# Graph network layer on one core: key, value and query products moved from the nodes in the last layer to the edges in attention

## Chip, cores and metric

One core of a Trainium2 chip runs the whole program in one launch. The metric is device time in microseconds, the median of a few runs; a profile is one more execution, read instruction by instruction. PE is the matrix engine, DVE the vector engine, ACT the scalar engine, POOL issues indirect transfers (gathers) and SP the plain ones.

## The reference, cut to what matters

```python
def L0(h, incidence, W_edge, b_edge, W_agg, b_agg):      # 3 rounds
    for _ in range(3):
        msgs = relu(take(h, src) @ W_edge + b_edge)
        agg = segment_sum(msgs, dst)
        h = relu(concat([agg, h]) @ W_agg + b_agg)
    return h
def L1(x, edge_index, edge_attr, ...):                   # H = 8 heads of C = 16
    q, k, v = x @ Wq + bq, x @ Wk + bk, x @ Wv + bv
    e = edge_attr @ We
    k_j, v_j = k[src] + e, v[src] + e
    logits = sum(q[dst] * k_j, axis=-1) / sqrt(C)
    ex = exp(logits - segment_max(logits, dst)[dst])
    agg = segment_sum(ex / denom[dst] * v_j, dst)
    h = ln(agg + x @ Wskip + bskip + x, g1, b1)
    return ln(gelu(h @ Wf1 + bf1) @ Wf2 + bf2 + h, g2, b2)
x = layernorm(x + L0(x, ...))
return layernorm(x + L1(x, edge_index, edge_attr_64, ...))
```

There are 50,000 nodes and 50,000 edges, sorted by dst; x has 128 columns, all fp32. Below, x1 is the x of the second-last line.

## The kernel before

The program runs in stages with a barrier between them: sorting, message passing (two rounds), the last layer (the third round and the first layer norm), a short table stage, attention, and feed-forward. A group is 512 rows (98 groups), a block 256 nodes (196 blocks).

`last_layer` works block by block. Each engine has a `turn(do)`: `do(-8, group(step))` runs step for the block 8 before the present one, and `group` only in every second block, which closes a group. Engines run their lists in order and meet only at semaphores (`reached` is a wait). POOL gathers message rows of 768 bytes, four tiles a group, into a ring of 32 tiles; DVE makes one-hot matrices (`hots`, three a block); PE adds the tiles by them (`add_tile`), adds the node's own product (L1157), transposes the sums (`turn_sums`, L1164); DVE adds x (`add_rows`, L1264: y, four buffers) and takes means and variances (`norm_stats`); ACT takes the root (`roots`, L1205), DVE makes scale and shift in five small operations (`deviations`, L1270 to L1280), ACT normalizes (L1212); PE transposes x1 (`turn_x1`, L1171), ACT copies the columns (L1219), and PE projects them to 384 columns, keys, values and queries, for each of four tiles (`project`, L1181 and L1182). Half of these go through DVE with the bias (`add_biases`, L1292), half through ACT (`evict`, L1225). SP stores x1 plus b2, the columns of x1, and kvq_rows of 1536 bytes a node.

`attention` works group by group, by `do(lag, step)` too. POOL gathers for each of four tiles of 128 edges the kvq row of src (`at_kv`) and the q part of dst's (`at_q`). PE makes the edge features in rows (`e_bank`), DVE adds keys and values, multiplies by q, and sums each head (`edge_logits`); ACT spreads the logits over the head's 16 columns, PE transposes them and the values. With edges along the free axis DVE then scans for the running maximum (`maxima`), `weigh`s the values, and scans numerator and denominator (`num_scan`, `den_scan`); PE transposes back (`turn_back`), DVE divides. PE also makes x1 @ (Wskip + I) here from the stored columns (`skip_product`), and between steps multiplies a constant tile (`keep_busy`, L1431), four products at three places of a turn, whose result is not used.

## Time and profile before

| | |
|---|---|
| Runs | 4398.65, 4410.13, 4412.01 us (median 4410.13) |
| Profiled execution, span from first to last instruction | 4405.3 us; this is the time of its own that the profile gives |
| Busy over the span | PE 3865.1, DVE 3498.7, POOL 2905.4, ACT 2233.6 us |
| Transferred | 878.32 MB, 199 GB/s on average |

Busy times overlap and are averages over stages with different limits; the same figures for one stage, and the order in time within one group, tell what that stage waits for. A matrix product's record includes its tail, so starts are compared with starts.

### The profile page before, as it was taken

The numbers are of one execution on the slowest core, as the hardware profiler recorded it, in microseconds if no ns is written. First come the engines' busy times: TensorE is split into PE (matmuls) and PEld (weight loads), VectorE is DVE, ScalarE is ACT, GpSimd is POOL, SyncE is SP. The second block draws the span as 40 slices with busy tenths as digits, with TensorE's granted clock in tenths as the row PEclk, the third lists the DMA queues.
The fourth block names the chain that finished last, engine by engine and source line by source line (L and its number), as shares of the span: only waits on it lengthen the run. The fifth ranks groups of instructions, "written<-read, shape, count | busy, mean of one in ns | idle before, by whom it ended". The sixth has DMA issues, their size and how long they took to land. (4 is left out here: it accounts for less than half of the span.)

```text
span 4405.3 us, 106270 instructions
## 1 busy us (share of the span) xinstructions
PE 3865.1 (88%) x21528; PEld 2669.2 (61%) x21627; DVE 3498.7 (79%) x11629; ACT 2233.6 (51%) x4904; POOL 2905.4 (66%) x2864
## 2 busy tenths in 40 slices
PE   5777769999899997999999788888889859999998
PEld 3555548878788886566666466666666634444443
DVE  7888857766567665788877689999999958999998
ACT  1333335555455553455554444444444437777777
POOL 3777767776477763655555177777777657777775
PEclk9999989999999999999999889888888979999999
DMA  2555558877578775788888667777777624444443
GB/s 88 174 176 176 176 162 244 246 234 235 183 241 244 236 234 177 263 303 301 293 298 283 236 192 207 204 205 208 207 207 203 186 86 125 132 126 132 126 131 94
DMA packets 610107, 878.32 MB, mean 199 GB/s; under 512 B 148009, under 2 KB 409232, under 8 KB 609932
## 3 DMA queue, kind: packets, MB, share of 16 engines
q1 hardware_dynamic: 490764, 631.93, 43.6%
q0 software_dynamic: 119168, 244.63, 21.5%
q14 instruction: 135, 1.11, 0.1%
q8 instruction: 40, 0.66, 0.1%
HBM read 477.60 MB, written 398.61 MB: 199 GB/s over the span
## 5 line engine op out<-in xcount | busy, mean ns | idle before, releaser
L798 POOL DMA_INDIRECT mp_gathered<-msg_rows,other_idx x784 | 754.6, 962 | 348.7 <-issue 198.8
L1120 POOL DMA_INDIRECT ll_gathered<-msg_rows,other_idx x392 | 385.0, 982 | 357.0 <-PE bank L1138 204.4
L816 PE MATMUL bank<-mp_edge_hot,mp_gathered 128*128 128x256 bf16 x3528 | 475.5, 275 | 34.5 <-POOLq L786 18.3
L560 POOL DMA_INDIRECT by_window<-so_pay,so_pos_i x392 | 387.1, 988 | 164.3 <-issue 111.3
L1713 POOL DMA_INDIRECT ff_agg<-at_rows,last_idx x392 | 383.2, 978 | 116.0 <-issue 105.9
L1415 POOL DMA_INDIRECT at_kv<-kvq_rows,kv_idx x392 | 377.2, 962 | 119.7 <-issue 112.4
L1417 POOL DMA_INDIRECT at_q<-kvq_rows,node_idx x392 | 376.5, 960 | 119.5 <-issue 117.1
L872 ACT ACTIVATE mp_h_out<-bank,mp_b_agg 128x256 f32<-128x256 f32 x392 | 185.9, 474 | 476.9 <-PE bank L834 469.6
L816 PEld LDWEIGHTS bank<-mp_edge_hot,mp_gathered 128*128 x3528 | 346.3, 98 | 104.4 <-issue 61.7
L905 DVE TENSOR_SCALAR mp_edge_hot<-digits,mp_first_col,column 128x256 bf16<-128x256 bf16 x1176 | 342.0, 359 | 66.5 <-issue 54.5
L928 DVE TENSOR_TENSOR mp_msg_out<-mp_rest,mp_msg_out 128x256 bf16<-128x256 f32 x392 | 166.8, 426 | 259.1 <-ACT mp_msg_out L885 255.4
L1825 PE MATMUL bank<-ff_h_cols,ff_w 128*128 128x512 f32 x784 | 371.2, 596 | 0.9 <-ACT ff_h_cols L1858 0.9
L1833 PE MATMUL bank<-ff_gelu,ff_w 128*128 128x512 f32 x784 | 369.6, 594 | 1.0 <-ACT ff_gelu L1865 1.0
L1431 PE MATMUL bank<-at_filler,ones 128*128 128x512 bf16 x1078 | 320.7, 421 | 20.2 <-issue 15.3
L1182 PE MATMUL bank<-ll_weights,ll_x_cols 128*128 128x384 f32 x784 | 323.5, 515 | 0.0
L1865 ACT ACTIVATE ff_gelu<-bank,ff_bf 128x512 f32<-128x512 f32 x392 | 262.5, 683 | 114.6 <-PE bank L1825 114.6
L1726 POOL TENSOR_TENSOR ff_rstd<-ff_eps_var,ff_half 128x12 f32<-128x12 f32 x104 | 239.4, 2302 | 107.7 <-DVE ff_eps_var L1749 104.0
L1825 PEld LDWEIGHTS bank<-ff_h_cols,ff_w 128*128 128x128 f32 x784 | 149.9, 191 | 189.9 <-issue 188.4
L1138 PE MATMUL bank<-ll_edge_hot,ll_gathered 128*128 128x256 bf16 x1764 | 236.6, 274 | 25.4 <-DVE ll_edge_hot L1245 23.4
L834 PE MATMUL bank<-mp_h_in,mp_w_agg_h 128*128 128x256 f32 x784 | 245.8, 396 | 9.3 <-issue 8.8
L845 PEld LDWEIGHTS bank<-mp_w_agg_a,mp_msg_cols 128*128 128x128 f32 x1568 | 237.9, 192 | 21.8 <-ACT mp_msg_cols L876 1.2
L845 PE MATMUL bank<-mp_w_agg_a,mp_msg_cols 128*128 128x128 f32 x1568 | 239.4, 275 | 0.9 <-DVE mp_rest L923 0.9
(267 smaller groups left out, 9434.1 us busy)
## 6 DMA issues: line engine op xcount, KB each, us to landing
msg_rows<-mp_msg_out SPq DMA_DIRECT2D x392, 192.0 KB
kvq_rows<-ll_proj SPq DMA_DIRECT2D x98, 768.0 KB
mp_h_in<-h_cols SPq DMA_DIRECT2D x392, 128.0 KB
h_cols<-mp_h_out SPq DMA_DIRECT2D x392, 128.0 KB
msg_rows<-so_msg_out SPq DMA_DIRECT2D x98, 384.0 KB
h_cols<-so_h_out SPq DMA_DIRECT2D x98, 256.0 KB
ll_h_in<-h_cols SPq DMA_DIRECT2D x196, 128.0 KB
x_rows<-ll_x_b SPq DMA_DIRECT2D x98, 256.0 KB
```

The source lines that it names most:

```text
L560: pool.indirect_dma_start(core.by_window, bass.IndirectOffsetOnAxis(ap=pos_i[k][:, t:t + 1], axis=0), pay[k][:, t, :], None, bounds_check= ...
L798: pool.indirect_dma_start(gathered[:, r * PARTS * D:(r + 1) * PARTS * D], None, core.msg_rows[layer % 2], bass.IndirectOffsetOnAxis(ap=cor ...
L816: product = nc.tensor.matmul(agg_bank[k], gathered[:, bass.ds(at + d * D, D)], hot, start=(first and d == 0), stop=True, skip_group_check= ...
L845: product = nc.tensor.matmul(msg_bank[r % 2][:, c * P:(c + 1) * P], msg_c[r % 2][:, c * P:(c + 1) * P], w_agg_a[:, :], start=True, stop=True)
L905: return nc.vector.tensor_scalar(to, core.digits[:, :], first_col[:, bass.ds(n, 1)], core.column[:, bass.ds(i, 1)], ALU.add, ALU.is_equal)
L1120: pool.indirect_dma_start(gathered[:, r * PARTS * D:(r + 1) * PARTS * D], None, core.msg_rows[(LAYERS - 1) % 2], bass.IndirectOffsetOnAxis ...
L1182: nc.tensor.matmul(proj_bank[t][:, 0:NPJ], x1_cols[q % 2][:, t * P:(t + 1) * P], weights[:, :], start=t < T - BY_ACT, stop=True, skip_grou ...
L1415: pool.indirect_dma_start(kv[g % DEEP][:, t, :], None, core.kvq_rows, bass.IndirectOffsetOnAxis(ap=core.kv_idx[:, at:at + 1], axis=0)).the ...
L1417: pool.indirect_dma_start(q[g % DEEP][:, t, :], None, core.kvq_rows.rearrange("n (a f) -> (n a) f", f=D), bass.IndirectOffsetOnAxis(ap=cor ...
L1713: pool.indirect_dma_start(agg[g % 4][:, t, :], None, core.at_rows, bass.IndirectOffsetOnAxis(ap=core.last_idx[:, at:at + 1], axis=0)).then ...
L1825: nc.tensor.matmul(hid_bank[c][:, :], w1[:, c * P:(c + 1) * P], h_c[k % 2][:, :], start=True, stop=True).then_inc(f1, 1)
L1833: product = nc.tensor.matmul(out_bank[k % 2][:, :], w2[:, c, :], act_c[c][:, :], start=(c == 0), stop=(c == FC - 1))
```

## The change

The last layer no longer projects to keys, values and queries. Its place is taken by the skip product, which came from attention; x1 is stored without b2, its columns are no longer stored. `roots` and `deviations` run once for two groups (`pair`), and normalization and what follows it run two groups later. Attention gathers rows of x1 (512 bytes) for src and for dst, transposes them on PE, and makes keys, values and queries for each edge with edges along the free axis: keys and values each as two accumulating products (`with_edges`, x1 of src and edge attributes). DVE multiplies keys plus bias by queries (`products`), and one product with a 0/1 matrix of heads (`logits`) sums each head and spreads the sum. `keep_busy` is gone. DVE also adds b2 to x1 here and SP stores it for the feed-forward stage. The decay goes to SBUF instead of PSUM. The rest of the stages is unchanged but for the names of tensors.

```diff
+        def pair(step):
+
+            def at_fourth_block(n, r, j):
+                if r % 4 == 3:
+                    step(PAIRS * j + r // 4, r // 4)
+            return at_fourth_block
+
         words = {}
...
             def store(g):
-                k = g % 2
-                reached(sp, xb2_ok, g + 1)
-                sp.dma_start(rows(core.x1_rows, g), x1_b2[k][:, :, :]).then_inc(st_x1[k], 16)
-                reached(sp, cols_ok, g + 1)
-                sp.dma_start(core.x1_cols[:, g * GR:(g + 1) * GR], x1_cols[k][:, :]).then_inc(st_cols[k], 16)
-                reached(sp, by_act, BY_ACT * (g + 1))
-                reached(sp, by_dve, (T - BY_ACT) * (g + 1))
-                sp.dma_start(rows(core.kvq_rows, g), proj[k][:, :, :]).then_inc(st[k], 16)
+                reached(sp, x1_ok, g + 1)
+                sp.dma_start(rows(core.x1_rows, g), x1[g % Q][:, :, :]).then_inc(st_x1[g % Q], 16)
+                reached(sp, skip_ok, g + 1)
+                sp.dma_start(rows(core.skip_rows, g), skip[g % 2][:, :, :]).then_inc(st_skip[g % 2], 16)
 
             for n in range(RING - 1):
                 load_h(n)
...
+            def skip_product(g, q, j):
                 pe.wait_ge(cols_ok, g + 1)
+                reached(pe, skip_ok, g - 1)
+                nc.tensor.matmul(skip_bank[q % 2][:, :], core.ones[0:PARTS, :], skip_parts[:, :], start=True, stop=True, skip_group_check=True)
                 for t in range(T):
-                    if t < T - BY_ACT:
-                        reached(pe, by_dve, (T - BY_ACT) * (g - 1) + t + 1)
-                    else:
-                        reached(pe, by_act, BY_ACT * (g - 1) + t - (T - BY_ACT) + 1)
-                        nc.tensor.matmul(proj_bank[t][:, 0:NPJ], core.ones[0:PARTS, :], proj_parts[:, :], start=True, stop=True, skip_group_check=True)
-                    nc.tensor.matmul(proj_bank[t][:, 0:NPJ], x1_cols[q % 2][:, t * P:(t + 1) * P], weights[:, :], start=t < T - BY_ACT, stop=True,
-                                     skip_group_check=True).then_inc(mm, 1)
+                    last = nc.tensor.matmul(skip_bank[q % 2][:, t * P:(t + 1) * P], x1_cols[q % 2][:, t * P:(t + 1) * P], w_skip[:, :],
+                                            start=False, stop=True, skip_group_check=True)
+                last.then_inc(skip_mm, 1)
 
             def turn(do):
                 do(0, sum_edges)
                 do(-2, group(turn_sums))
-                do(-8, group(turn_x1))
-                do(-10, group(project))
+                do(-12, group(turn_x1))
...
             def normalize(g, q, j):
-                act.wait_ge(rstd_ok, g + 1)
+                act.wait_ge(rstd_ok, PAIRS * j + q // 2 + 1)
                 reached(act, x1_t, g - Q + 1)
-                reached(act, xb2_ok, g - Q + 1)
...
                 do(0, group(close_group))
-                do(-4, group(roots))
-                do(-8, group(x1_columns))
-                do(-6, group(normalize))
-                do(-10, group(evict))
+                do(-6, pair(roots))
+                do(-12, group(x1_columns))
+                do(-10, group(normalize))
+                do(-14, group(skip_copy))
             blocks(act, turn)
...
             def turn(do):
                 do(-5, group(add_rows))
-                do(-8, group(deviations))
-                do(-10, group(add_b2))
-                do(-12, group(add_biases))
+                do(-8, pair(deviations))
                 do(0, hots)
...
-            def gather(g):
-                reached(pool, prod_ok, g - DEEP + 1)
-                reached(pool, ve_ok, g - DEEP + 1)
-                reached(pool, e_mm, g - DEEP + 2)
...
+                               base=C - 1, pattern=[[C, H], [0, C]], channel_multiplier=-1).then_inc(setup, 1)
+
+            for g in range(NG):
+                reached(pool, src_t, g - DEEP + 1)
+                reached(pool, dst_t, g - DEEP + 1)
                 for t in range(T):
                     at = g * T + t
-                    pool.indirect_dma_start(kv[g % DEEP][:, t, :], None, core.kvq_rows,
-                                            bass.IndirectOffsetOnAxis(ap=core.kv_idx[:, at:at + 1], axis=0)).then_inc(g_in[g % DEEP], 16)
-                    pool.indirect_dma_start(q[g % DEEP][:, t, :], None, core.kvq_rows.rearrange("n (a f) -> (n a) f", f=D),
-                                            bass.IndirectOffsetOnAxis(ap=core.node_idx[:, at:at + 1], axis=0)).then_inc(g_in[g % DEEP], 16)
-
-            for g in range(NG):
-                gather(g)
+                    pool.indirect_dma_start(of_src[g % DEEP][:, t, :], None, core.x1_rows,
+                                            bass.IndirectOffsetOnAxis(ap=core.kv_idx[:, at:at + 1], axis=0)).then_inc(src_in[g % DEEP], 16)
+                for t in range(T):
+                    at = g * T + t
+                    pool.indirect_dma_start(of_dst[g % DEEP][:, t, :], None, core.x1_rows,
...
+            def turn_src(g, k, i):
+                pe.wait_ge(src_in[k], 64 * (i + 1))
+                reached(pe, src_ok, g)
+                for t in range(T):
+                    last = nc.tensor.transpose(src_bank[:, t * P:(t + 1) * P], of_src[k][:, t, :], ident[:, :])
+                last.then_inc(src_t, 1)
+
+            def turn_dst(g, k, i):
+                pe.wait_ge(dst_in[k], 64 * (i + 1))
+                pe.wait_ge(a_ok, g + 1)
+                for t in range(T):
+                    last = nc.tensor.transpose(turn_bank[:, t * P:(t + 1) * P], of_dst[k][:, t, :], ident[:, :])
+                last.then_inc(dst_t, 1)
 
...
+            def with_edges(to, weights, k):
+                nc.tensor.matmul(to[:, :], weights[:, :], src_cols[k][:, :], start=True, stop=False)
+                return nc.tensor.matmul(to[:, :], w_e[:, :], attr_cols[k][:, :], start=False, stop=True)
+
+            def keys(g, k, i):
+                pe.wait_ge(src_ok, g + 1)
+                pe.wait_ge(a_ok, g + 1)
                 reached(pe, prod_ok, g)
-                keep_busy(e_bank)
+                with_edges(key_bank, w_k, k).then_inc(key_mm, 1)
+
+            def queries(g, k, i):
+                pe.wait_ge(dst_ok, g + 1)
+                reached(pe, query_ok, g)
+                nc.tensor.matmul(query_bank[:, :], w_q[:, :], dst_cols[k][:, :], start=True, stop=True).then_inc(query_mm, 1)
+
+            def values(g, k, i):
+                pe.wait_ge(src_ok, g + 1)
                 pe.wait_ge(a_ok, g + 1)
-                for t in range(T):
-                    last = nc.tensor.matmul(e_bank[:, t * P:(t + 1) * P], attr_cols[k][:, t * P:(t + 1) * P], w_e[:, :],
-                                            start=True, stop=True)
-                last.then_inc(e_mm, 1)
-
...
+            def logits(g, k, i):
+                pe.wait_ge(prod_ok, g + 1)
                 reached(pe, step_ok, g)
-                pe.wait_ge(spread_ok, g + 1)
-                keep_busy(logit_bank)
-                for t in range(T):
-                    last = nc.tensor.transpose(logit_bank[:, t * P:(t + 1) * P], spread[k][:, t, :], ident[:, :])
-                last.then_inc(log_t, 1)
-
...
             def turn(do):
-                do(2, turn_attr)
-                do(1, edge_features)
-                do(-1, turn_values)
-                do(-2, turn_back)
-                do(0, skip_product)
-                do(0, turn_logits)
+                do(-2, logits)
+                do(-4, turn_back)
+                do(0, turn_src)
+                do(-1, keys)
+                do(-1, queries)
+                do(-3, values)
+                do(0, turn_dst)
+                do(1, turn_attr)
...
             def turn(do):
-                do(-1, skip_copy)
+                do(0, src_copy)
+                do(-1, query_copy)
+                do(0, dst_copy)
+                do(-2, exponentials)
+                do(0, breaks)
                 do(1, attr_copy)
-                do(0, spread_logits)
-                do(0, breaks)
-                do(-1, exponentials)
             turns(act, turn, DEEP, 8)
 
         @block.vector
...
+            def products(g, k, i):
+                dve.wait_ge(key_mm, g + 1)
+                dve.wait_ge(query_ok, g + 1)
+                reached(dve, logit_mm, g - 1)
+                nc.vector.scalar_tensor_tensor(out=prod[k][:, :], in0=key_bank[:, :], scalar=b_k[:, 0:1], in1=query[k][:, :],
+                                               op0=ALU.add, op1=ALU.mult).then_inc(prod_ok, 1)
+
+            def add_b2(g, k, i):
+                dve.wait_ge(x1_in[k], 16 * (i + 1))
+                reached(dve, st_b2[(k + 2) % DEEP], 16 * (i + (k - 2) // DEEP + 1))
+                nc.vector.tensor_tensor(x1_b2[k][:, :, :], x1[k][:, :, :], b2[:, :].unsqueeze(1).broadcast_to([P, T, D]), ALU.add).then_inc(xb2_ok, 1)
+
+            def weigh(g, k, i):
...
             def turn(do):
-                do(0, edge_logits)
-                do(-2, weigh)
-                do(-2, num_scan)
-                do(-2, den_scan)
-                do(-1, maxima)
-                do(-3, divide)
+                do(-2, maxima)
+                do(0, add_b2)
+                do(-4, divide)
+                do(-1, products)
+                do(-3, weigh)
+                do(-3, den_scan)
+                do(-3, num_scan)
             turns(dve, turn, DEEP, 8)
```

On PE in the last layer, at the end of a group (a late one, after the loop), before:

```order
L1157 MATMUL bank<-ll_h_in,ll_w_agg_h 128x256
L1164 MATMUL bank<-ident,ll_sums 128x128 x4
L1171 MATMUL bank<-ident,ll_x 128x128 x4
L1182 MATMUL bank<-ll_weights,ll_x_cols 128x384 x2
L1181 MATMUL bank<-ll_proj_parts,ones 128x384
L1182 MATMUL bank<-ll_weights,ll_x_cols 128x384
L1181 MATMUL bank<-ll_proj_parts,ones 128x384
L1182 MATMUL bank<-ll_weights,ll_x_cols 128x384
```

and now:

```order
L1156 MATMUL bank<-ll_h_in,ll_w_agg_h 128x256
L1163 MATMUL bank<-ident,ll_sums 128x128 x4
L1170 MATMUL bank<-ident,ll_x 128x128 x4
L1176 MATMUL bank<-ll_skip_parts,ones 128x512
L1178 MATMUL bank<-ll_w_skip,ll_x_cols 128x128 x4
```

Behind the two sets of transposes stood six products for the projection; now a product for the bias and four of 128 columns stand there.

On PE in attention, one turn, before (bank names are left out by the listing; at_filler is the constant tile):

```order
L1431 MATMUL bank<-at_filler,ones 128x512 x4
L1446 MATMUL bank<-at_we,at_attr_cols 128x128 x4
L1431 MATMUL bank<-at_filler,ones 128x512 x4
L1463 MATMUL bank<-ident,at_v_e 128x128 x4
L1471 MATMUL bank<-ident,at_num 128x128 x4
L1473 MATMUL bank<-at_pick,at_den 128x8 x4
L1479 MATMUL bank<-at_skip_parts,ones 128x512
L1481 MATMUL bank<-at_wskip,at_x_cols 128x128 x4
L1431 MATMUL bank<-at_filler,ones 128x512 x4
L1455 MATMUL bank<-ident,at_spread 128x128 x4
L1438 MATMUL bank<-ident,at_attr 64x128 x4
```

and now:

```order
L1465 MATMUL bank<-at_prod,at_heads 128x512
L1472 MATMUL bank<-ident,at_num 128x128 x4
L1474 MATMUL bank<-at_pick,at_den 128x8 x4
L1423 MATMUL bank<-ident,at_of_src 128x128 x4
L1442 MATMUL bank<-at_src_cols,at_wk 128x512
L1443 MATMUL bank<-at_attr_cols,at_we 128x512
L1454 MATMUL bank<-at_dst_cols,at_wq 128x512
L1442 MATMUL bank<-at_src_cols,at_wv 128x512
L1443 MATMUL bank<-at_attr_cols,at_we 128x512
L1430 MATMUL bank<-ident,at_of_dst 128x128 x4
```

Products with at_wk, at_wv and at_wq of 512 columns take the place of the constant ones; turn_back (L1472, L1474) stands ahead of them, the transposes of the dst rows and attributes behind.

On DVE in attention, one turn, before:

```order
L1557 TENSOR_TENSOR at_v_e<-at_kv,bank 128x512
L1560 TENSOR_TENSOR bank<-at_kv,bank 128x512
L1563 TENSOR_TENSOR at_prod<-at_q,bank 128x512
L1566 TENSOR_REDUCE at_logits<-at_prod 128x32
L1573 TENSOR_TENSOR at_weighted<-bank,at_weight 128x512
L1581 SCALAR_TENSOR_TENSOR at_num<-bank,at_num,at_weighted 128x512
L1590 SCALAR_TENSOR_TENSOR at_den<-bank,at_den,at_weight 128x512
L1597 SCALAR_TENSOR_TENSOR at_top<-at_break,at_top,bank 128x512
L1601 TENSOR_TENSOR at_drop<-at_top,at_break 128x512
L1602 COPY at_top<-at_top 128x1
L1606 TENSOR_TENSOR at_step<-at_drop,bank 128x512
L1611 TENSOR_SCALAR at_inv<-bank 128x32
```

and now, where the first row is the scan of the maximum:

```order
L1552 SCALAR_TENSOR_TENSOR at_top<-at_break,at_top,bank 128x512
L1556 TENSOR_TENSOR at_drop<-at_top,at_break 128x512
L1557 COPY at_top<-at_top 128x1
L1561 TENSOR_TENSOR at_step<-at_drop,bank 128x512
L1573 TENSOR_TENSOR at_x_b<-at_x,at_b 128x512
L1603 TENSOR_SCALAR at_inv<-bank 128x32
L1605 RECIPROCAL at_inv<-at_inv 128x32
L1608 TENSOR_TENSOR at_rows<-bank,at_inv 128x512
L1567 SCALAR_TENSOR_TENSOR at_prod<-bank,at_bk,at_query 128x512
L1579 SCALAR_TENSOR_TENSOR at_weighted<-bank,at_bv,at_weight 128x512
L1588 SCALAR_TENSOR_TENSOR at_den<-at_decay,at_den,at_weight 128x512
L1597 SCALAR_TENSOR_TENSOR at_num<-at_decay,at_num,at_weighted 128x512
```

The first four operations of before's list (v_e, key, product, sum per head) are gone, two are new (L1567, L1573), and the three scans stand apart: maximum first, denominator and numerator last.

## Rows read from the trace of the kernel before

**Rows 1.** The page's head.

```profile
span 4405.3 us, 106270 instructions
```

**Rows 2.** Windows of the last layer and of attention; columns as the first row says.

```profile
core 0: us, PE busy (x) PEld busy (x) DVE busy (x) ACT busy (x) POOL busy (x), PEclk, DMA share, GB/s
...
1725.00:2500.00 775.00, 740.19 (x3944) 467.22 (x3944) 591.33 (x2273) 376.13 (x881) 384.99 (x392) 0.98 0.83 281
2500.00:3545.00 1045.00, 886.49 (x5098) 640.99 (x5195) 939.87 (x1391) 421.05 (x787) 753.93 (x786) 0.87 0.70 198
```

**Rows 3.** The last layer's gathered tile: PE products, ns min/median/max, first and last start.

```profile
L1138 PE MATMUL bank<-ll_edge_hot,ll_gathered x1764: 272/273/417, 1743.6 to 2475.9; 128*128 128x256 bf16 x196
```

**Rows 4.** Timeline of PE, last layer: start, duration (us), what.

```profile
2104.16 0.60 PE L1171 MATMUL bank<-ident,ll_x 128*128 128x128 f32 x4
2104.59 1.46 PE L1182 MATMUL bank<-ll_weights,ll_x_cols 128*128 128x384 f32 x4
...
2108.10 1.15 PE L1138 MATMUL bank<-ll_edge_hot,ll_gathered 128*128 128x256 bf16 x9
...
2111.80 1.46 PE L1182 MATMUL bank<-ll_weights,ll_x_cols 128*128 128x384 f32 x4
```

**Rows 5.** The tiles at_kv and at_q: POOL's gathers.

```profile
L1415 POOL DMA_INDIRECT at_kv<-kvq_rows,kv_idx x392: 945/949/1465, 2515.7 to 3505.9; - x196
...
L1417 POOL DMA_INDIRECT at_q<-kvq_rows,node_idx x392: 941/947/1464, 2516.9 to 3507.1; - x196
```

**Rows 6.** Windows of 100 us, attention.

```profile
2900.00:3000.00 100.00, 90.19 (x506) 65.05 (x513) 91.61 (x137) 42.16 (x80) 75.91 (x80) 0.85 0.73 208
```

**Rows 7.** Timeline of PE, attention.

```profile
3008.98 0.66 PE L1471 MATMUL bank<-ident,at_num 128*128 128x128 f32 x4 [1.63 <-DVE at_rows L1616]
...
3010.36 0.39 PE L1479 MATMUL bank<-at_skip_parts,ones 3*128 3x512 bf16 x1
...
3011.67 1.03 PE L1431 MATMUL bank<-at_filler,ones 128*128 128x512 bf16 x4
...
3018.77 0.66 PE L1471 MATMUL bank<-ident,at_num 128*128 128x128 f32 x4 [1.73 <-DVE at_rows L1616]
...
3021.05 2.08 PE L1481 MATMUL bank<-at_wskip,at_x_cols 128*128 128x128 f32 x8
```

**Rows 8.** DMA issues: count, KB each.

```profile
kvq_rows<-ll_proj SPq DMA_DIRECT2D x98, 768.0 KB
```

**Rows 9.** Timeline of all engines, last layer.

```profile
2101.38 0.38 SPq L1080 DMA_DIRECT2D x_rows<-ll_x_b  x1
...
2104.98 0.69 DVE L1286 TENSOR_TENSOR ll_x_b<-ll_x,ll_b 128x512 f32<-128x512 f32 x1 [1.34 <-DMA x_rows<-ll_x_b]
...
2105.62 0.60 ACT L1219 ACTIVATE ll_x_cols<-bank 128x512 f32<-128x512 f32 x1 [0.75 <-DMA x_cols<-ll_x_cols]
...
2106.11 1.64 ACT L1212 ACTIVATE ll_x<-ll_y,ll_shift,ll_rstd 128x128 f32<-128x128 f32 x4
...
2107.34 0.68 DVE L1264 TENSOR_TENSOR ll_y<-bank,ll_x_in 128x512 f32<-128x512 f32 x1
...
2109.50 0.86 DVE L1245 TENSOR_SCALAR ll_edge_hot<-digits,ll_first_col,column 128x256 bf16<-128x256 bf16 x3
...
2110.27 0.17 DVE L1270 RECIPROCAL ll_inv<-ll_root 128x4 f32<-128x4 f32 x1
...
2111.85 0.69 DVE L1286 TENSOR_TENSOR ll_x_b<-ll_x,ll_b 128x512 f32<-128x512 f32 x1 [0.61 <-DMA x_rows<-ll_x_b]
```

**Rows 10.** Timeline of PE in the feed-forward stage.

```profile
4001.68 2.74 PE L1833 MATMUL bank<-ff_gelu,ff_w 128*128 128x512 f32 x6
4004.26 2.74 PE L1825 MATMUL bank<-ff_h_cols,ff_w 128*128 128x512 f32 x6
```

**Rows 11.** The tile ff_z_cols: DVE, PSUM plus scalar and a second operand.

```profile
L1764 DVE SCALAR_TENSOR_TENSOR ff_z_cols<-bank,ff_bf,ff_h_cols x98: 750/751/752, 3596.7 to 4383.8; 128x512 f32<-128x512 f32 x98
```

**Rows 12.** Timeline of DVE, attention.

```profile
3002.63 1.28 DVE L1581 TENSOR_TENSOR_SCAN at_num<-bank,at_num,at_weighted 128x512 f32<-128x512 f32 x1
```

356 lines of the change are left out of this document (159 added, 197 removed).

## Prediction

> **What bounds the kernel now.** I read the page's head [rows 1] and then the windows by stage [rows 2]: the changed code is in two of five stages, the last layer (775 us with the gaps around it) and attention (1,045 us).
>
> In the last layer PE is busy 740 of 775 us at a granted clock of 0.98, DVE 591, ACT 376, POOL 385. From the first edge product to the last are 732 us [rows 3], 7.48 us for each of 98 groups. The PE timeline [rows 4] shows a group without a stall: from the projection's start (2104.59) to the next edge products (2108.10) 3.51 us, from there over two blocks and two sets of transposes to the next projection (2111.80) 3.70 us, together 7.21. The missing 0.27 us is further tiles, branches and the cold start. PE is the bound.
>
> In attention POOL issues 784 gathers in 991.4 us from the first start to the last [rows 5]: 1.266 us each, 10.13 us a group of eight. In 100 us it is busy 75.9 [rows 6], the rest being the 0.30 us between gathers: it hardly ever waits and sets the stage. DVE is close behind at 91.6, PE at 90.2 with its fillers and a clock of 0.85.
>
> **Last layer, part by part.** PE loses the projection, 3.51 us a group. It gets the skip product, a 3-row bias product and four products of 128 columns; attention has the same five now, from 3010.36 to the filler at 3011.67, 1.31 us [rows 7]. So 3.70 + 1.31 + 0.27 = 5.28 us a group.
>
> DVE loses two bias additions, the b2 addition and half of five small operations a group, ACT two copies of 384 columns for one of 512: neither is the bound, both get less, so this is worth 0 by itself. POOL needs 4 x 1.266 = 5.06 us a group; idle half the time now, it becomes the floor of this stage, just under PE.
>
> A group moves four gathers of 98 KB, 262 KB of h, 262 KB of x and two stores of 262 KB, 1.44 MB, where it also stored 786 KB of kvq [rows 8]. At 5.28 us that is 273 GB/s, and the stage carries 281 on average today [rows 2]. I take it as hidden.
>
> Two loops are late next. *First*, normalization moves from lag -6 to -10. y has four buffers, so add_rows(g) waits for normalization of g-4, which now runs in the turn in which PE transposes the sums of g. From the end of PE's x1 transposes (0.60 after 2104.16) [rows 4]: ACT's copy 0.60 and normalization 1.64; on DVE y, stats and moments 2.16, three hots 0.77, in every second group the small operations 0.97 (2110.27 to 0.61 before 2111.85), three hots 0.86 [rows 9]; then PE's block 1.4 (3.70 less two sets of transposes, by two), its transposes 0.44 and 0.60. That is 9.4 us for two groups, 4.7 a group. *Second*, SP waits for that y before it issues load_x and the h of three blocks ahead, and then stands at the store of skip_rows until ACT's copy. An h load issued 4.4 us after the end of a block (transposes 0.9, copy 0.6, normalization 1.6, y 0.7, SP's issues 0.5) is wanted 1.5 groups later, and half a group (2.0 us with a full block) follows; so two groups hold 4.4 + latency + 2.0 us. The latency of a 256 KB store under this load is 3.6 us (issued 2101.38, its waiter starts 2104.98) [rows 9]; with that, 5.0 a group. Both loops lie 0.3 to 0.6 under 5.28, so now and then they will bite; I take 5.35. The roots at lag -6 and the chain at -8 leave PE a tail of 2.2 us to cover one root and the chain; without that cover they are one of the small terms of the first loop.
>
> So the last layer gives (7.48 - 5.35) x 98 = -209 us. Its drain is two groups longer (lag -14 for -10) but each group costs ACT's 2.8 us (0.6 + 1.6 + 0.6) and no 3.5 us projection: 7 x 3 against some 26 us from the last edge product to the stage's end, -5. Bounds: POOL's floor of 5.06 gives -237, both loops biting always at 5.9 gives -155.
>
> **Attention, part by part.** The gathers stay eight a group. at_kv moves rows of 1536 B, at_q rows of 512 B, and POOL's medians are 949 and 947 ns [rows 5], so smaller rows buy POOL nothing: 10.13 us stay. DVE loses four operations of 0.7 us for two; nobody waits for that, worth 0.
>
> The Trainium skill (DMA: Bandwidth & Descriptors, "Anatomy of one DMA — SWDGE (gpsimd) path") fits such a transfer at 2.0 us plus its bytes over 436 GB/s, so that the four kv gathers would each shorten by 0.3 us. By that estimate the stage would gain 118 us if POOL waited for its transfers; the rows have it not waiting, and the sum takes 0.
>
> PE's real work grows. A group has fp32 products of 512 columns: logits 1, keys 2, queries 1, values 2. Three take 2.58 us (4001.68 to 4004.26), 0.86 each [rows 10]. With three sets of transposes at 0.44 [rows 4] and turn_back at 1.38 (3008.98 to 3010.36) [rows 7] it is 5.16 + 1.32 + 1.38 = 7.86 us at full clock. The loop through it is longer: after values(g-3), DVE's weigh 0.75 [rows 11], two scans of 1.28 [rows 12] and 0.1 of handover, 3.4 together; then, since PE runs in order, turn_back 1.38, transposes 0.44, keys 1.72, queries 0.86, values 1.72, so 6.12. Sum 9.5 us, under POOL's 10.13 by 0.6. At a mean granted clock c it is 3.4 + 6.12/c: 10.13 at c = 0.91, 10.6 at 0.85.
>
> Which c? The slow stretch at 3021.05 came after PE had idled 1.73 us for DVE and then done only transposes and eight-column products [rows 7]. The fillers (12 products a group, four in 1.03 us with their tail) go, but real products take their place, and the wait for the scans shortens: PE has 2.4 us of other steps (two sets of transposes, ACT's copy between them, logits) beside the 3.4, which leaves 1.0. I take c near 0.92, so 10.13 with a little over it: +4 us. POOL begins 1 us later (two more selects); the drain stays within 5 us.
>
> **Sum** against the profiled span: -209 - 5 + 4 + 1 = -209, so 4405 - 209 = 4196. The median of the runs is 4.8 us above that span: 4200. Within 0.3% (13 us) is about what a measurement of this kernel cannot tell from no change.
>
> **Rivals.**
> *Attention goes over to PE (0.20).* The loop at c = 0.85, which is today's clock in [rows 6], gives 10.6 us, +46: about 4240. Against it: shorter idle stretches.
> *The last layer is held by its loops or transfers (0.14).* For it: 0.3 to 0.6 us of slack over four engines and a DMA latency. At 5.9 us a group: 4255.
> *Gathers get cheaper (0.04).* If POOL's pace followed bytes, attention would fall to the loop at 9.5: 0.6 x 98 = 59 us less, 4140. Against it: 949 and 947 ns. The page cited above bears on this one.
> *The kernel gets slower (0.03).* The place is PE's clock in attention without fillers. At the lower level throughout, 3.4 + 12.24 = 15.6 us a group, +540: about 4740. It decides from +209 us on, 12.3 us a group, c = 0.69. The 2.08 us of the four skip products at 3021.05, against 1.31 at 3010.36 for the same with their bias product, show what that level costs [rows 7]. Against it: a slow PE is busy all the time, and before's came back to full speed.
> The Trainium skill (TensorE: Matmul & The Clock Gate, "What's actually happening") says that the low clock is the default and that activity lifts it. It speaks against taking the fillers out; the slow stretch behind an idle one [rows 7] agrees with it.
> *The change does little (0.01).* PE would not be the last layer's bound; 740 of 775 us speak against it.
> The forecast has 0.58, with a range of its own of 4170 to 4222.
>
> **Range.** Below lie POOL's floor in the last layer (4172) and cheaper gathers (4140, 0.04); above, 4240 and 4255. From 4152 to 4265 I leave out the ends, about 2 in 10. Faster 0.96, same 0.01, slower 0.03.
>
> **What would show it.** Right: last layer near 5.35 us a group, PE over 90% and POOL with its gaps near 95% busy; attention with POOL still at 75.9 of 100 us, DVE near 85, clock at 0.9 or more, PE waiting about 1 us for a scan. Wrong: POOL waiting in attention for a transpose of of_src or of_dst (the loop is over 10.13); a clock under 0.85; in the last layer PE waiting for ll_edge_hot behind a ll_y that ACT's normalization released, or for ll_h_in.

## The result, and the profile after

The changed kernel takes 4299.9 us (median of 4 runs, 4291.8 to 4302.9), the kernel before 4405.1 (4 runs, 4398.7 to 4412.0): a ratio of 0.9756, 95% interval 0.9738 to 0.9774. The forecast was 4200 with a range of 4152 to 4265. The sign was right, the size was not: about half of the 209 us came.

The head of the changed kernel's page [before: rows 1]:

```profile
span 4301.0 us, 101522 instructions
```

Windows of the changed kernel: the last layer, attention, and 100 us inside each [before: rows 2, 6].

```profile
core 0: us, PE busy (x) PEld busy (x) DVE busy (x) ACT busy (x) POOL busy (x), PEclk, DMA share, GB/s
...
1728.00:2396.00 668.00, 603.83 (x3849) 428.71 (x3849) 415.25 (x1736) 334.10 (x736) 372.29 (x392) 0.97 0.67 212
2396.00:3440.00 1044.00, 891.95 (x3530) 434.08 (x3530) 811.39 (x1186) 487.42 (x883) 752.27 (x789) 0.97 0.50 148
...
2000.00:2100.00 100.00, 95.35 (x620) 67.77 (x619) 65.61 (x272) 54.26 (x120) 58.37 (x62) 1.00 0.71 229
2900.00:3000.00 100.00, 88.76 (x361) 42.94 (x359) 82.00 (x121) 49.56 (x90) 75.89 (x80) 1.00 0.52 156
```

The changed kernel's tiles: the last layer's edge products on PE with POOL's wait for them (us, times), then attention's two gathers on POOL [before: rows 3, 5].

```profile
L1137 PE MATMUL bank<-ll_edge_hot,ll_gathered x1764: 272/273/421, 1741.8 to 2370.7; 128*128 128x256 bf16 x196
...
PE bank L1137: 114.0, 76
```

```profile
L1407 POOL DMA_INDIRECT at_of_src<-x_rows,kv_idx x392: 940/945/1777, 2407.0 to 3390.8; - x196
...
L1411 POOL DMA_INDIRECT at_of_dst<-x_rows,node_idx x392: 940/945/1944, 2412.0 to 3395.9; - x196
```

Attention did what was forecast: POOL's gathers run from 2407.0 to 3395.9, 988.9 us against 991.4 [rows 5], with POOL at 75.9 of 100 us and DVE at 82. The last layer did not. Its edge products span 628.9 us, 6.42 a group, against 732.3 before and 524 (5.35 a group) forecast: 105 us too much, where the whole run missed by 100. I call this span, from the start of the first always-taken edge product to that of the last, *the stage*.

The DMA share fell from 0.83 to 0.67, and POOL, which was to be the next floor, waits 114.0 us for PE's products, so neither transfers nor gathers hold it. PE reads as 95.35 of 100 us busy at full clock, with nearly a third of its work gone. The changed kernel's PE timeline shows how:

```profile
2110.29 1.71 PE L1137 MATMUL bank<-ll_edge_hot,ll_gathered 128*128 128x256 bf16 x9
2112.12 0.70 PE L1156 MATMUL bank<-ll_h_in,ll_w_agg_h 128*128 128x256 f32 x2
2112.66 0.60 PE L1163 MATMUL bank<-ident,ll_sums 128*128 128x128 f32 x4
2113.09 0.60 PE L1170 MATMUL bank<-ident,ll_x 128*128 128x128 f32 x4
2113.62 0.39 PE L1176 MATMUL bank<-ll_skip_parts,ones 3*128 3x512 bf16 x1
2113.94 1.16 PE L1178 MATMUL bank<-ll_w_skip,ll_x_cols 128*128 128x128 f32 x8
2114.93 1.15 PE L1137 MATMUL bank<-ll_edge_hot,ll_gathered 128*128 128x256 bf16 x9
...
2116.35 1.15 PE L1137 MATMUL bank<-ll_edge_hot,ll_gathered 128*128 128x256 bf16 x9
2117.54 0.70 PE L1156 MATMUL bank<-ll_h_in,ll_w_agg_h 128*128 128x256 f32 x2
```

The nine edge products of a block took 0.98 us from their start to that of the h product before (2108.10 to 2109.08; the 1.15 in [rows 4] holds the tail). Here the same nine take 1.83 (2110.29 to 2112.12) or 1.19 (2116.35 to 2117.54), with no idle time shown between them. Taken over all blocks between 1900 and 2250 us, the second block of a group takes 1.71 us in the mean (over 50 of them) against 1.14 before, the first 1.19 against 0.98. The Trainium skill (Perfetto Trace Analysis, its introduction) calls matmul busy time a bad metric, because matmuls are pipelined. This trace agrees that it misleads: of the 6.36 us that a group takes in this window, 0.91 are such stretching (1.71 + 1.19 + 0.49 + 0.54 for two blocks with their h products, where 3.02 before), and all of it reads as busy.

What lies between the products is not in the profile, but in the program. TensorE's instructions from the skip product to the end of the next block, in order; an address that stands in a register costs an ISA instruction ahead of each product, a tile some REGISTER_ALU, and a branch follows:

```
L1178 MATMUL bank<-ll_w_skip,ll_x_cols 128x128 x4
L1149 REGISTER_ALU
L1150 REGISTER_ALU x2
L1137 REGISTER_ALU
L1137 ISA
L1137 MATMUL bank<-ll_edge_hot,ll_gathered 128x256
L1137 ISA
L1137 MATMUL bank<-ll_edge_hot,ll_gathered 128x256
L1137 ISA
L1137 MATMUL bank<-ll_edge_hot,ll_gathered 128x256
L1137 REGISTER_ALU x2
...
L1055 REGISTER_ALU
L1055 COMPARE_AND_BRANCH
```

The single starts follow this pattern. In the blocks of over 1.7 us (51 of them between 1900 and 2250 us) products start 0.12 to 0.13 us apart within a tile, 0.32 from a tile's last to the next tile's first, and 0.42 from the ninth to the h product. In blocks of 0.98 us all these distances are 0.11.

So the first theory (S): TensorE's instruction stream works these off one by one. While the array had 3.51 us of projection to do, the stream could get that far ahead; behind a 1.31 us skip product it can't. The rivals: the array's own work (A), and waits in the loop of the moved steps (B), which the changed kernel's waits suggest. DVE's idle time before the first operation of the deviations, and before y (us, times):

```profile
ACT ll_root L1202: 66.8, 46
...
ACT ll_x L1209: 82.6, 74
```

### The profile page after: what moved, and what is told of

The parts are those of the page before. It is cut to its first block and busy times, and to the rows that moved or that the text cites. A ratio compares the mean times of both kernels' runs of the same rounds, so it can differ in the third digit from the quotient of the medians.

```text
span 4301.0 us, 101522 instructions
## 1 busy us (share of the span) xinstructions
PE 3741.4 (87%) x19862; PEld 2424.7 (56%) x19863; DVE 3192.7 (74%) x10886; ACT 2257.7 (52%) x4855; POOL 2889.9 (67%) x2867
## 3 DMA queue, kind: packets, MB, share of 16 engines
q1 hardware_dynamic: 476652, 554.66, 39.8%
## 5 line engine op out<-in xcount | busy, mean ns | idle before, releaser
L1119 POOL DMA_INDIRECT ll_gathered<-msg_rows,other_idx x392 | 372.3, 950 | 268.1 <-PE bank L1137 114.0
L1411 POOL DMA_INDIRECT at_of_dst<-x_rows,node_idx x392 | 377.9, 964 | 119.5 <-issue 119.5
L1407 POOL DMA_INDIRECT at_of_src<-x_rows,kv_idx x392 | 373.3, 952 | 119.3 <-issue 119.0
L1137 PE MATMUL bank<-ll_edge_hot,ll_gathered 128*128 128x256 bf16 x1764 | 273.4, 279 | 30.1 <-DVE ll_edge_hot L1242 19.4
L1137 PEld LDWEIGHTS bank<-ll_edge_hot,ll_gathered 128*128 x1764 | 171.9, 97 | 125.8 <-issue 89.8
L838 PE MATMUL bank<-mp_h_out,mp_w_edge 128*128 128x256 f32 x784 | 236.1, 383 | 0.0
```

The source lines that it names most:

```text
L1119: pool.indirect_dma_start(gathered[:, r * PARTS * D:(r + 1) * PARTS * D], None, core.msg_rows[(LAYERS - 1) % 2], bass.IndirectOffsetOnAxis ...
L1137: product = nc.tensor.matmul(block_sums(r), gathered[:, bass.ds(at + d * D, D)], hot, start=(first and d == 0), stop=True, skip_group_chec ...
L1407: pool.indirect_dma_start(of_src[g % DEEP][:, t, :], None, core.x1_rows, bass.IndirectOffsetOnAxis(ap=core.kv_idx[:, at:at + 1], axis=0)). ...
L1411: pool.indirect_dma_start(of_dst[g % DEEP][:, t, :], None, core.x1_rows, bass.IndirectOffsetOnAxis(ap=core.node_idx[:, at:at + 1], axis=0) ...
```

## Experiments

Lags are blocks behind the block that an engine has reached. Each edit is on the changed kernel, if nothing else is said. Two executions of the changed kernel itself had stages of 628.9 and 633.7 us (the second is the one timed last, below), so differences of some 5 us between single runs say nothing. Both places earlier (below) had 575.6 and 576.4. Only the runs with the root earlier, with both places earlier and with the changed kernel again were timed several times; every other time is one execution, and every stage length is that of one profile. Leaving the skip product out (500 us by A, 560 to 617 by S) was meant as one more test of A; it gave no result.

**Cover.** Two long products more a group.

```diff
+                for _ in range(2):
+                    nc.tensor.matmul(bank[5][:, :], w_skip[:, :], x1_cols[q % 2][:, :], start=True, stop=True, skip_group_check=True)
                 for t in range(T):
                     last = nc.tensor.matmul(skip_bank[q % 2][:, t * P:(t + 1) * P], ...
```

> Two more fp32 products of 512 columns per group on TensorE, into an unused bank, ahead of the four skip products of the last layer; nothing reads them. At 0.86 us each (the price of such products before) they are 1.72 us of array work in a group, with few instructions around them. Measure: from the first to the last edge product of the last layer, 628.9 us in the changed kernel, 6.42 a group. Theory S (TensorE's instruction stream, the register and branch instructions around the edge products, is what the group takes, and long products only hide it): 6.4 to 6.7 a group, 630 to 660 us. Rival A (the array's own work fills the group): 6.42 + 1.72 = 8.1, about 797 us. Rival B (the loop of adds, root, deviations and normalization holds the pace, with TensorE waiting in it): 6.4 to 6.9, since only the waits would be filled.

Its edge products, and a group on its PE timeline:

```profile
L1137 PE MATMUL bank<-ll_edge_hot,ll_gathered x1764: 272/273/421, 1738.3 to 2427.5; 128*128 128x256 bf16 x196
```

```profile
2108.07 1.05 PE L1180 MATMUL bank<-ll_w_skip,ll_x_cols 128*128 128x128 f32 x8
2108.96 1.15 PE L1137 MATMUL bank<-ll_edge_hot,ll_gathered 128*128 128x256 bf16 x9
2109.94 0.60 PE L1156 MATMUL bank<-ll_h_in,ll_w_agg_h 128*128 128x256 f32 x2
2110.38 1.15 PE L1137 MATMUL bank<-ll_edge_hot,ll_gathered 128*128 128x256 bf16 x9
2111.36 0.60 PE L1156 MATMUL bank<-ll_h_in,ll_w_agg_h 128*128 128x256 f32 x2
```

The stage takes 689.2 us, 7.03 a group: +60 us for the 169 us of array work that was put in. That lies between S (up to 660) and A (797). The timeline shows why it is so cheap: both blocks are back at 0.98 us (in the mean over 1900 to 2250, first 0.98, second 1.15, as before the change). About 0.9 us a group of stretching went, 1.7 us of product came. S is right about the blocks; that it would be nearly free was too much. This run alone doesn't part S from the waits: at 7.03 us a group the one-hots too are done earlier, 1.9 us or more ahead of every block in that window (0.4 in the changed kernel). The next run does. The idle time of the weight loads ahead of the edge products that nothing in the profile explains ("issue", last number) fell with it, from 89.8 us in the changed kernel (60.5 before the change) to 35.5:

```profile
L1137 PEld LDWEIGHTS bank<-ll_edge_hot,ll_gathered 128*128 x1764 | 171.9, 97 | 125.8 <-issue 89.8
```

```profile
L1137 PEld LDWEIGHTS bank<-ll_edge_hot,ll_gathered 128*128 x1764 | 173.0, 98 | 69.0 <-issue 35.5
```

**Fixed address.**

```diff
-                    product = nc.tensor.matmul(block_sums(r), gathered[:, bass.ds(at + d * D, D)], hot, ...
+                    product = nc.tensor.matmul(block_sums(r), fixed[:, d * D:(d + 1) * D], hot, ...
```

> The products of the always-taken and further edge tiles read one fixed tile of zeros instead of the gathered tile whose address stands in a register; the waits for the gathers, the one-hots and the number and shape of the products stay. The sums are therefore those of h alone. Measure as in the first: 628.9 us now. Theory S: with the address arithmetic gone the two blocks of a group take 1.41 us or less each and the group 5.3 to 5.6 us, 520 to 550 us. Rivals A and B: no change, 620 to 635 us.

```profile
L1139 PE MATMUL bank<-ll_edge_hot,ll_fixed x1764: 272/273/421, 1740.0 to 2280.1; 128*128 128x256 bf16 x196
```

540.1 us, 5.51 a group, with the same number and shape of products: S, inside its bounds. A alone is out. The tile is of zeros, but that gave no faster array: the granted clock between 1900 and 2250 us is 1.00 here and in the changed kernel, and the products' median is 273 ns in both.

**As before.** The steps of the small operations back to their old places, and for each group apart.

```diff
-                if r % 4 == 3:
-                    step(PAIRS * j + r // 4, r // 4)
+                if r % 2:
+                    step(Q * j + r // 2, r // 2)
...
-                do(-6, pair(roots))
-                do(-12, group(x1_columns))
-                do(-10, group(normalize))
-                do(-14, group(skip_copy))
+                do(-4, pair(roots))
+                do(-8, group(x1_columns))
+                do(-6, group(normalize))
+                do(-10, group(skip_copy))
```

> The changed kernel with the root and the chain of deviations again for each group apart, and all the steps of the last layer at the places that they had before (roots 4 blocks behind, normalization 6, transposes and copy 8, skip product and its copy 10; stores 5 groups behind). Only what the change took out of the last layer stays out. Theory S: TensorE has the same instructions, so 6.3 to 6.5 a group, 620 to 640 us. Rival B, with the shared root and the later places as its cause: below 6.1, under 600 us. If sharing and later places did bring something (fewer operations on VectorE, shorter waits), over 650 us.

Its edge products, and what DVE waited for ahead of the deviations:

```profile
L1137 PE MATMUL bank<-ll_edge_hot,ll_gathered x1764: 272/273/421, 1742.1 to 2318.0; 128*128 128x256 bf16 x196
```

```profile
ACT ll_root L1202: 0.2, 1
```

575.9 us, 53 less than the changed kernel, and 4235.9 us for the whole. S alone (620 to 640) did not expect this: TensorE has the same instructions. So the blocks are stretched by two things, and half of the shortfall lies in the sharing or in the new places of root, normalization and what follows them.

Four runs tell its parts apart: each group apart but at the new places; two banks for the transposed sums; the sharing kept, with the normalization (and what follows it) two blocks earlier; and PE's x1 steps behind a group's first block.

```diff
-                    reached(pe, y_ok, g)             # two banks for the sums
+                    reached(pe, y_ok, g - 1)
...
-                do(-10, group(normalize))            # sharing kept, earlier
+                do(-8, group(normalize))
...
-                do(-12, group(turn_x1))              # spread
-                do(-14, group(skip_product))
+                do(-12, group_early(turn_x1))
+                do(-14, group_early(skip_product))
```

> The changed kernel with the root and the chain of deviations for each group apart again, and all steps at the new, later places. With the run that also had the old places (575.9 us from the first to the last edge product of the last layer, against 628.9 in the changed kernel) it tells the two halves of the move apart. Theory L (the later places cost it: the normalization of group g-4 stands 10 blocks behind on ScalarE, VectorE's y of group g waits for its buffer, and the one-hots that TensorE's instruction stream needs next stand behind it): 610 to 640 us. Rival P (the sharing costs it: two groups must be done before the root, and one chain stands in one place): 570 to 590 us.

> The changed kernel with two banks for the transposed sums instead of one, so that TensorE's transposes of group g wait for y of group g-2 instead of g-1; all places stay. Theory L (TensorE's instruction stream is held at the wait for the one-hots): 615 to 632 us, no gain. Rival R (it is held at the wait for y, ahead of the transposes of the sums): 570 to 600 us.

> The changed kernel, with the shared root and deviations where they are, and the normalization 8 blocks behind instead of 10, the transposes and copy of x1 10 instead of 12, the skip product and its copy 12 instead of 14, stores 6 groups instead of 7. Theory L: the y buffer comes free a block or two earlier, 570 to 595 us. Rival P (the sharing costs it, not the places): 615 to 640 us, or more, since the normalization now waits for deviations that have just been made.

> The changed kernel with TensorE's transposes of x1 and skip product behind the first block of a group instead of the second (12 and 14 blocks behind still, one block later in time), so that each of the two register-heavy blocks has array work ahead of it: transposes of sums and the bias come before one, the skip product before the other. Theory S (instruction stream needs cover): second blocks fall from 1.71 us towards 1.1, first ones rise from 1.19 to at most 1.4; the stage 590 to 620 us. If TensorE's stream is held mostly by the wait for one-hots, no change: 620 to 640 us.

The edge products of the four in this order, one fence each, and behind the third what its DVE waited for ahead of the deviations:

```profile
L1137 PE MATMUL bank<-ll_edge_hot,ll_gathered x1764: 272/280/421, 1741.5 to 2375.9; 128*128 128x256 bf16 x196
```

```profile
L1137 PE MATMUL bank<-ll_edge_hot,ll_gathered x1764: 272/273/422, 1744.4 to 2368.7; 128*128 128x256 bf16 x196
```

```profile
L1137 PE MATMUL bank<-ll_edge_hot,ll_gathered x1764: 272/273/422, 1743.9 to 2367.0; 128*128 128x256 bf16 x196
```

```profile
ACT ll_root L1202: 128.4, 48
```

```profile
L1144 PE MATMUL bank<-ll_edge_hot,ll_gathered x1764: 272/273/421, 1740.9 to 2420.4; 128*128 128x256 bf16 x196
```

634.4, 624.3, 623.1 and 679.5 us. The first clears the sharing: apart or together, the stage is the same. The second clears the single bank. The third refutes my theory L in the form in which it stood, that the late normalization alone was to blame: with it earlier, DVE's wait for y is gone (0.8 us) and the wait for the root has grown from 66.8 to 128.4. The fourth was a miss by both its theories: TensorE got a wait of its own, for x1, 34.1 us ahead of the transposes, and waited 42.1 us for one-hots ahead of the edge products, against 19.4 in the changed kernel (the "early" steps stand a block earlier in time, not later as I had written).

That gives theory D. An in-order engine that waits at lag *a* for a step which another does at lag *b* can lead it by *a - b* blocks. ACT runs with PE (its relu waits for the block). DVE's deviations (8) wait for the root: a lead of 8 - 4 = 4 before, 8 - 6 = 2 now. y of group g (5) waits for the normalization of g-4, eight blocks earlier: 5 + 8 - 6 = 7 before, 5 + 8 - 10 = 3 now. y waits for the transposed sums: 5 - 2 = 3 in both. By theory D the smallest counts, and one-hots made two blocks ahead come so late that TensorE's stream is held for them. The changed kernel's timeline of ACT and DVE shows one turn of it:

```profile
2112.86 0.69 ACT L1197 ACTIVATE ll_sums<-bank,ll_agg_bias 128x512 f32<-128x512 f32 x1 [3.81 <-PE bank L1156]
...
2114.22 1.64 ACT L1209 ACTIVATE ll_x<-ll_y,ll_shift,ll_rstd 128x128 f32<-128x128 f32 x4
...
2115.99 0.69 DVE L1261 TENSOR_TENSOR ll_y<-bank,ll_x_in 128x512 f32<-128x512 f32 x1 [3.23 <-ACT ll_x L1209]
...
2118.15 0.86 DVE L1242 TENSOR_SCALAR ll_edge_hot<-digits,ll_first_col,column 128x256 bf16<-128x256 bf16 x3
...
2120.36 0.86 DVE L1242 TENSOR_SCALAR ll_edge_hot<-digits,ll_first_col,column 128x256 bf16<-128x256 bf16 x3
```

and PE's blocks for which these one-hots are:

```profile
2120.35 1.15 PE L1137 MATMUL bank<-ll_edge_hot,ll_gathered 128*128 128x256 bf16 x9
...
2121.80 1.68 PE L1137 MATMUL bank<-ll_edge_hot,ll_gathered 128*128 128x256 bf16 x9
2123.63 0.70 PE L1156 MATMUL bank<-ll_h_in,ll_w_agg_h 128*128 128x256 f32 x2
```

DVE stands 3.23 us for ACT, and the next one-hots are done at 2119.01. TensorE's array doesn't stop; it is at the transposes (2118.07 and 2118.51) and the skip product behind them. The block of these one-hots starts 1.34 us after they are done and still takes 0.98. The one-hots of the block behind it are done at 2121.22; it starts 0.58 us later and takes 1.83. Its stream had no lead left, and every register instruction shows. How often that happens is counted below.

**The root's place alone, and with the normalization's; a wider lead all round.**

```diff
-                do(-6, pair(roots))                  # first: this line alone
+                do(-4, pair(roots))
...
-                do(-10, group(normalize))            # second: this as well, and its followers
+                do(-8, group(normalize))
...
-                do(-5, group(add_rows))              # third: instead of both, with two banks for the sums
-                do(-8, pair(deviations))
+                do(-7, group(add_rows))
+                do(-10, pair(deviations))
```

> The changed kernel with one number different: the shared root stands 4 blocks behind on ScalarE instead of 6. Theory D (VectorE's deviations stand 8 behind and wait for the root, so VectorE can be at most 8 - 6 = 2 blocks ahead of ScalarE, which itself waits for TensorE's block of the same number; before it was 8 - 4 = 4; with so little lead the one-hots come just in time and TensorE's instruction stream loses the cover under which it works off its register instructions): with 4 the bound is the y buffer's, 5 + 8 - 10 = 3 blocks, and that of the transposed sums, 5 - 2 = 3, so 575 to 605 us from the first to the last edge product of the last layer, and the whole 25 to 55 us below the changed kernel's 4300. Rival L (the later normalization is to blame): 620 us or more, the whole within 10 us of 4300.

> The one before with the normalization 8 blocks behind instead of 10 as well, transposes and copy of x1 10, skip product and its copy 12, stores 6 groups. The limit by the y buffer is 5 blocks instead of 3. Theory D: as the one before or a little better, 565 to 590 us, since the transposed sums still allow 3 blocks. A rival in which the normalization waits for deviations just made: above the one before by 10 us or more.

> The changed kernel with all steps on ScalarE and TensorE where they are, and on VectorE the adds 7 blocks behind instead of 5 and the deviations 10 instead of 8, with two banks for the transposed sums (without the second the transposes would wait for an add that stands later), and the loads of x one group later. VectorE's lead may then be 4 by the root, 5 by the transposed sums, 5 by y. Theory D: the widest lead of all, 540 to 575 us. If lead isn't what matters: 615 us or more.

The edge products of the three, and behind each of the first two what DVE waited for ahead of y:

```profile
L1137 PE MATMUL bank<-ll_edge_hot,ll_gathered x1764: 272/273/421, 1741.7 to 2350.1; 128*128 128x256 bf16 x196
```

```profile
ACT ll_x L1209: 133.2, 85
```

```profile
L1137 PE MATMUL bank<-ll_edge_hot,ll_gathered x1764: 272/273/421, 1741.5 to 2317.1; 128*128 128x256 bf16 x196
```

```profile
PE bank L1163: 87.9, 77
```

```profile
L1137 PE MATMUL bank<-ll_edge_hot,ll_gathered x1764: 272/273/421, 1747.5 to 2316.9; 128*128 128x256 bf16 x196
```

608.4 us (a little above D's 575 to 605), 575.6 and 569.4, the latter two as expected. The third also has the loads of x a group later. The whole took 4279.0 us with the root alone (median of 4 runs, 4277.5 to 4279.5; ratio 0.9717, 0.9701 to 0.9733), 21 us below 4300 where D had 25 to 55. The wait moves as D says: from the root to y's buffer, from there to the transposed sums. With the block times of the PE timeline between 1900 and 2250 us (first block to its h product, h, second block to its h product, h; means, added):

| kernel | lead by root, y, sums | stage, us | two blocks, us |
|---|---|---|---|
| before | 4, 7, 3 | 732.3 | 3.02 |
| changed | 2, 3, 3 | 628.9 | 3.93 |
| normalization earlier | 2, 5, 3 | 623.1 | 3.86 |
| root earlier | 4, 3, 3 | 608.4 | 3.79 |
| both | 4, 5, 3 | 575.6 | 3.46 |
| apart, old places | 4, 7, 3 | 575.9 | 3.46 |
| wider | 4, 5, 5 | 569.4 | 3.40 |

Neither step alone gives the 53 us, together they do. That the smallest lead alone counts is not borne out: 3 is the smallest with the root earlier and with both, and they are 33 us apart. My reading, not shown by a run, is that the lead by y counts for less than its 3 says: the normalization comes last in ACT's turn, the transposes early in PE's. Beyond 4, 5, 3 more lead brings next to nothing.

The means hide where in a loop the blocks are stretched. A pass of the loop has eight blocks; by their place in it (us from the first edge product to the h product, 1900 to 2250 us, blocks without further tiles; the last row is a run that follows below):

| kernel | 0 | 1 | 2 | 3 | 4 | 5 | 6 | 7 |
|---|---|---|---|---|---|---|---|---|
| before | 0.98 | 1.56 | 0.98 | 1.04 | 0.98 | 0.98 | 0.98 | 1.00 |
| changed | 1.88 | 1.81 | 0.98 | 1.84 | 0.98 | 1.37 | 0.98 | 1.79 |
| both earlier | 1.63 | 1.81 | 0.98 | 1.14 | 0.98 | 1.15 | 0.98 | 1.11 |
| one address of three | 1.05 | 1.02 | 0.98 | 0.98 | 0.98 | 0.98 | 0.98 | 1.00 |

The two earlier places mend blocks 3 and 7 above all. In the changed kernel these start 0.52 and 0.60 us in the mean after the last of their one-hots is done, and 0.43 is the least that any block has; with both places earlier they start 4.5 and 3.0 us after. So there TensorE was held at the one-hots, as D says. Blocks 0 and 1 remain at 1.63 and 1.81, though their one-hots are done 2.7 and 4.0 us ahead. That is not lead. The branch back and the load of the pass's tile counts stand in the stream before block 0; that these use up the cover fits, but no run takes them out.

**Fixed address with the root earlier**, the edits of two runs above together.

> The root 4 behind, as in the first of this call, and the fixed tile of zeros in place of the address held in a register, as in the second experiment (the sums are those of h alone). With either alone known, this tells whether the two causes are one: if the short lead costs only because it uncovers the register instructions, the fixed tile's 540.1 us can hardly fall, 520 to 540. If they add, the gain of the root's place comes on top, 540 - 35 to 540 - 50, about 490 to 505 us, below the gathers' own pace of 5.06 a group, 496 us, so held there.

```profile
L1139 PE MATMUL bank<-ll_edge_hot,ll_fixed x1764: 272/273/421, 1736.7 to 2271.3; 128*128 128x256 bf16 x196
```

534.6 us. With the address fixed, the root's place is worth 5.5 us, at the scatter; with the address in a register it was worth 20.5. The two causes don't add: a short lead costs mostly because it uncovers the register instructions. This run could not have shown much more, though: only 21 us lie between 540.1 and the 519.3 of the last experiment, where no stretching is left, so the 490 to 505 of the rival was out of reach. DVE still waited 64.4 us for the normalization ahead of y.

**What remains: spread with the lead restored, and fewer address instructions.** The first has the root at 4, the normalization at 8 and PE's x1 steps behind the first block. The second is on the kernel with both places earlier:

```diff
+                    tile = fixed[:, d * D:(d + 1) * D] if d else gathered[:, bass.ds(at, D)]
-                    product = nc.tensor.matmul(block_sums(r), gathered[:, bass.ds(at + d * D, D)], hot, ...
+                    product = nc.tensor.matmul(block_sums(r), tile, hot, ...
```

> TensorE's transposes of x1 and skip product behind the first block of a group, as in the spread before, but with the lead restored: the root 4 blocks behind, the normalization 8 (so the transposes of x1 come three blocks after it on the count instead of one). In the spread before, TensorE itself waited 34.1 us for x1 and the stage took 679.5 us. Theory S: each block has cover of its own, second ones fall from 1.31 us to about 1.1, and the stage takes 550 to 575 us against 575.6 with the same lead and no spread. If the waits that hold TensorE's instruction stream count for more than where the cover stands: 575 to 600 us.

> The kernel with root and normalization earlier (575.6 us), where only the first of the three products of a tile takes its weights at the address from the register and the other two read a fixed tile of zeros: a register-address instruction less for two products in three, 6 in a block, the address arithmetic of a tile kept; the low parts of the messages are left out of the sums. Theory S, every such instruction costing its time on the stream: the stage falls most of the way to the 534.6 us of the fixed tile, 540 to 555 us, and second blocks from 1.31 to about 1.2 us. If the arithmetic or the branches are the cost and not these: 565 to 577 us.

The edge products of the first; of the second, those with the fixed tile:

```profile
L1144 PE MATMUL bank<-ll_edge_hot,ll_gathered x1764: 272/273/421, 1738.6 to 2326.7; 128*128 128x256 bf16 x196
```

```profile
L1140 PE MATMUL bank<-ll_edge_hot,ll_fixed x1176: 272/273/421, 1739.7 to 2259.0; 128*128 128x256 bf16 x196
```

The spread takes 588.1 us, 12 more than without it. Second blocks, now behind the skip product, are at 0.99 us; first ones, with only the transposes of the sums ahead of them, are at 1.39. That is 0.08 us a group less than 1.15 and 1.31, but PE now waits 14.7 us for ACT's sums. So the place of the cover alone decides little here. One address instruction less for two products in three gives 519.3 us, 5.30 a group, below the 540 to 555 expected: blocks at 1.00 and 1.00 us, two with their h products 2.92. So six ISA instructions less in a block, with the address arithmetic and the branches kept, take out all the stretching that the restored lead had left, at the start of a pass as well (table above).

**Timed side by side**, on one chip: both places earlier, and the changed kernel again.

> The kernel with root 4 and normalization 8 behind, timed beside the next: about 4236 us, 60 to 68 us below the changed kernel and 3.7 to 4.0 per cent below the kernel before. By the rival that what was seen in single runs is scatter of the chip: within 15 us of the changed kernel.

> The changed kernel itself, timed on the same chip as the one before, to compare the two directly: 4295 to 4305 us, 2.3 to 2.6 per cent below the kernel before.

Both places earlier: 4239.7 us (median of 4, 4236.9 to 4248.4), ratio 0.9624, interval 0.9608 to 0.9640. The changed kernel: 4295.4 us (4289.8 to 4302.8), 0.9744, 0.9727 to 0.9760. The kernel before on that chip: 4406.3. So the two places, with the steps that follow them, are worth 56 us (60 to 68 were expected), and this version beats both kernels with the same arithmetic.

## Why the prediction was off

*The failed step* is "3.70 + 1.31 + 0.27 = 5.28 us a group", with "a full block" at 1.4 us in the loops. The terms were read rightly and 1.31 came nearly so: transposes, bias and skip product take 2.34 us together between 1900 and 2250 (0.44 + 0.53 + 0.32 + 1.05), where 0.87 + 1.31 = 2.18 was forecast. But 2.83 us for two blocks in [rows 4] is what they take *behind a projection*. Behind the skip product they take 3.93. That is 1.10 of the 1.14 us a group by which 6.42 exceeds 5.28. Not all of it came with the change: over many groups the kernel before has 3.02, and the 0.19 above the one group read was already in the sum, in its 0.27. The change brought 0.91. The projection was costed as array time to be removed; it was also what TensorE's instruction stream worked under. In the run with few address instructions and the lead restored the group takes 5.30 (2.92 for the blocks, 2.3 for the rest): the array sum was right, as the price of the array alone, though the near match is partly luck, with 2.18 too low and 0.27 hardly needed.

*The two loops* were named, and "both loops biting always at 5.9" was inside the range; but I asked only whether a loop takes longer than a group. At the 4.7 and 5.0 that I worked out they don't. What the new places do is shorten DVE's lead, and the loop that did most together with y's, root to deviations, was passed over in half a sentence ("one of the small terms"). Its lead went from 4 to 2 blocks through one number. Root and normalization at their late places cost 53 us of the 105; the other 50 to 56 are what remains with the lead restored, down to 519.3.

*Right*: projection removed, its time on PE; transfers hidden (share 0.67); the drain (from the last edge product to POOL's first gather 36.3 us, before 39.8; -5 and +1 forecast); POOL's pace independent of the row's size (945 and 945 ns for 512 B, 949 for 1536 B [rows 5]); attention at 988.9 us, where 991.4 + 4 was forecast. Copies and additions on DVE and ACT were taken as worth nothing; no run tests that by itself. Of the rivals none came: the clock did not hold attention (1.00 in the window, 0.97 in the stage, 0.92 forecast, 0.87 before), and "slower" by the missing fillers was far away, since longer real products took their place. The rival of a last layer held by its loops or transfers (5.9 a group, 4255) came nearest, but 6.42 lay beyond it, and half of its cause was not in it: it had the loops, but not the instruction stream.

*The sharing of root and chain* cost nothing and brought nothing that single runs show: 634.4 apart against 628.9 shared at late places, 575.9 against 575.6 at early ones.

*Small*: from POOL's last gather to the end took 905.1 us instead of 898.2; 5.6 of the 6.9 lie before the first ff_z_cols, which starts at 3491.1 us (before 3596.7 [rows 11]). I did not follow that up. The 4.8 us by which the median was taken to lie above the profiled span did not come again (4299.9 and 4301.0).

*Open*: no run varies one register instruction by itself. An estimate from the distances in the stretched blocks: a product with its ISA instruction 0.12 to 0.13 us, so about that for the ISA instruction; two REGISTER_ALU more between tiles 0.20, so about 0.10 each. A tile is then 0.57 us of stream against 0.33 of array, and with one address for three products 0.32, which just fits; that run agrees. That TensorE's stream is held at the one-hots is seen in where blocks 3 and 7 start, not in a row of its own; why blocks 0 and 1 are stretched is not shown.

## What to carry to other kernels

When long work is taken off an in-order engine, ask what its instruction stream was doing meanwhile: blocks with addresses in registers, branches and loads of counters are only as fast as the array if something long runs ahead of them. Their time should be read once behind a long product and once behind a short one before it is put in a sum. And for each wait between two engines, subtract the lags: a small difference is a short lead, and a loop that is short enough for the pace can still eat the lead. Then look at blocks by their place in the loop before averaging them: the first two of eight were slow for a reason of their own.

## What was unexpected

The same nine products take 0.98 us or up to 1.83 with hardly any idle time in the profile: PE reads 99.5 of 100 us busy before the change and 95.4 after it (2000 to 2100 us), though 0.91 of 6.36 us are stretching. The Trainium skill (Perfetto Trace Analysis, "Sequencer Loop") says that the sequencer pushes engine instructions into a queue but executes control instructions itself. The runs with cover (blocks at 0.98 us) and with fixed addresses (540.1 us) agree with it. In attention PE's granted clock rose from 0.85 to 1.00 [rows 6] although twelve filler products a group went; PE's busy share stayed about the same, 88.8 of 100 us against 90.2.
